# A decoder layer's first attention: three transposes by VectorE and a DRAM scratch in place of TensorE, and the output projection placed behind the diagonal blocks

## The reference

```python
q, k, v, g = x@Wq, x@Wk, x@Wv, x@Wg           # 16 heads; 64 columns of q and k, 128 of v and g a head
s = clip(x@Ws, -32, 32)                       # 64 slots a head
z = cumlogsumexp(s, time); p = exp(s - z); decay = exp(z_before - z)
hk = hk*decay + k (x) p;  ok = q*scale . hk   # a running state over the 512 tokens
pv = softmax(ok)                              # over the 64 slots
hv = hv*decay + p (x) v;  o = pv . hv
o  = o*rsqrt(mean(o*o)+eps)*g_norm*(g*sigmoid(g))
x  = layernorm(x + o@Wo)
```

## Time and profile before

| | us |
|---|---|
| median of 3 runs (1936.99 to 1939.8) | 1938.25 |
| profiled execution, whole | 1938.87 |
| profiled execution, span of the core | 1937.0 |
| PE busy in the span | 1905.9 (98%) |
| VectorE, ScalarE, POOL busy | 1235.6, 719.9, 555.9 |

### The profile page before, as it was taken

One profiled execution on the slowest core, in us unless ns is written; L12 is line 12 of the kernel. 1 busy time (PEld: TensorE's weight loads), 2 busy tenths in 40 slices (PEclk: granted clock), 3 DMA queues, 4 the chain that ended last, 5 costly groups with the idle time before them and its releaser, 6 DMA issues.

```text
span 1937.0 us, 30623 instructions
## 1 busy us (share of the span) xinstructions
PE 1905.9 (98%) x12099; PEld 1421.9 (73%) x12099; DVE 1235.6 (64%) x2107; ACT 719.9 (37%) x1819; POOL 555.9 (29%) x571
## 2 busy tenths in 40 slices
PE   9999999999999999999999989999999999999998
PEld 7888888888888888888888864444444468888876
DVE  4655555555555555555555678999999865555556
ACT  3222222222222222222222215888888832222122
POOL 2041151141141142142042243344242322223332
PEclk9999999999999999999999998999999999999999
DMA  5000100100001001001000001111110211111112
GB/s 174 1 1 12 39 11 2 39 12 24 16 12 39 1 12 39 1 12 39 1 12 4 6 2 26 27 27 27 27 27 20 34 19 22 30 20 30 20 17 87
DMA packets 124988, 47.08 MB, mean 24 GB/s; under 512 B 89264, under 2 KB 116400, under 8 KB 124848
## 3 DMA queue, kind: packets, MB, share of 16 engines
q1 hardware_dynamic: 124848, 45.14, 9.4%
HBM read 32.79 MB, written 4.19 MB: 19 GB/s over the span
## 4 chain that ended last, share of the span: by engine, by line
PE 92%; DVE 3%; ACT 3%; SPq 1%; issue 0%; DMA 0%; POOL 0%; POOLq 0%; DVEq 0%; ACTq 0%
PE a_ps L59 20%; PE a_ps L61 19%; PE a_ps L60 19%; PE a_ps L992 6%; PE a_ps L954 5%; PE a_ps L1008 5%; PE a_ps L1142 3%; PE a_ps L976 3%; PE a_ps L936 2%; ACT x_prob L1586 2%; PE a_ps L1087 2%; PE a_ps L1125 1%; PE a_ps L1068 1%; PE a_ps L1147 1%; PE a_ps L1130 1%; PE a_ps L1096 1%
## 5 line engine op out<-in xcount | busy, mean ns | idle before, releaser
L1650 DVE TENSOR_REDUCE a_raw_qks<-a_ps 128x1 f32<-128x512 f32 x512 | 320.9, 682 | 22.0 <-PE a_ps L954 21.3
L1586 ACT ACTIVATE x_prob<-a_ps 128x512 f32<-128x512 f32 x512 | 280.0, 609 | 63.4 <-PE a_ps L976 61.8
L1692 DVE SCALAR_TENSOR_TENSOR a_gate<-a_gate,a_ps 128x256 f32<-128x256 f32 x128 | 53.9, 421 | 264.0 <-ACT a_gate L1485 264.0
L1483 ACT COPY a_v<-a_ps 128x256 f32<-128x256 f32 x128 | 47.6, 372 | 436.5 <-PE a_ps L61 433.4
L59 PE MATMUL a_ps<-a_vg_hi,a_xT_lo 128*128 128x512 f32 x512 | 208.9, 408 | 0.0
L61 PE MATMUL a_ps<-a_vg_hi,a_xT_hi 128*128 128x512 f32 x512 | 200.9, 392 | 0.0
L60 PE MATMUL a_ps<-a_vg_lo,a_xT_hi 128*128 128x512 f32 x512 | 199.9, 391 | 0.0
L776 POOL TENSOR_TENSOR a_f<-a_rs 128x8 f32<-128x8 f32 x32 | 6.3, 198 | 569.9 <-ACT a_flat L1507 569.9
L59 PE MATMUL a_ps<-a_xT_hi,a_qks_lo 128*128 128x512 f32 x384 | 156.5, 408 | 0.4 <-DVE a_xT_lo L1681 0.4
L61 PE MATMUL a_ps<-a_xT_hi,a_qks_hi 128*128 128x512 f32 x384 | 150.0, 391 | 0.0
L60 PE MATMUL a_ps<-a_xT_lo,a_qks_hi 128*128 128x512 f32 x384 | 149.7, 390 | 0.0
(11 more groups left out here) (191 smaller groups left out, 4119.7 us busy)
## 6 DMA issues: line engine op xcount, KB each, us to landing
a_raw_vg<-in_L_attn_Wv_dram SPq DMA_DIRECT2D x8, 512.0 KB, 4.2
a_raw_vg<-in_L_attn_Wg_dram SPq DMA_DIRECT2D x8, 512.0 KB, 6.3
a_raw_qks<-in_L_attn_Wo_dram SPq DMA_DIRECT2D x8, 512.0 KB, 3.4
a_xT_lo<-a_xT_lo SPq DMA_DIRECT2D x32, 128.0 KB, 2.3
x_values<-acc SPq DMA_DIRECT2D x13, 256.0 KB, 2.8
acc<-in_x_dram SPq DMA_DIRECT2D x3, 1024.0 KB, 10.7
out_dram<-acc SPq DMA_DIRECT2D x6, 512.0 KB, 2.8
f_raw_down<-in_L_ffn_down_w_dram SPq DMA_DIRECT2D x44, 64.0 KB, 2.4
```

The lines of the kernel that those rows point to most:

```text
L1586: nc.scalar.activation(prob[par][:, s % 4, :], score_bank(q, s, par), ACT.Exp, scale=X_SCALE).then_inc(exp_done[par], 1)
L1650: nc.vector.tensor_reduce(nm[:, q % 2, i % 4, par, i // 4:i // 4 + 1], max_bank(u, q, i, par), AX.X, ALU.max, negate=True).then_inc(max_re ...
```

## The change

Transposes. For steps 1 to 31, e and the keys are no longer turned by PE. VectorE's transpose turns each block of 32x32 in place in one instruction (`turn_e` 512 columns, `turn_keys` 384). What is still missing is that the blocks change places; SP does that by writing to a DRAM tensor with four DMAs (one for each 32 rows, `put_blocks`) and reading it back with one (`get_blocks`), each waiting for the one before. ScalarE then reorders within a partition (`rows_of_e`, `rows_of_keys`). The gated output of steps 0 to 29 goes the same way in steps 1 to 30 (`turn_output`, 1024 columns; `put_og`, `get_og`, 512 KB each way; `high_turned` on ScalarE; `low_turned` on VectorE). Step 0's e and keys and the last two outputs stay with PE. SP's order within a step is put e, put keys, get e, put output, get keys, get output.

Order. On PE the projection K moves from behind the diagonal blocks to right behind S, and with it its copy on ScalarE; VG+3 comes ahead of the diagonal blocks and `project_out` behind them, ahead of Q. On VectorE `low_turned` stands ahead of the last gating, and `add_out` behind the masking of the diagonal blocks.

Weights. The factor of half the norm weight is multiplied into Wo by POOL (one more pass in `split_wo`), no longer into the output by ScalarE and VectorE; K and Q are split one by one; the load of Wo is issued in the fourth step of a pair.

The last two steps. Maxima of the second attention go to other PSUM banks; in `last_step` the eleven transposes of `keep_clock` ahead of `slots` and their wait are gone, and the row statistics of batch 2 are spread over that step instead of standing ahead of it.

The diff, cut to its core:

```diff
@@ SP, in place of the loop over pairs
+            def put_blocks(dram, turn, done):
+                for r in range(4):
+                    sp.dma_start(dram[:, :, r, :].rearrange("s j x -> j s x"),
+                                 turn[32 * r:32 * (r + 1), :, :, :].rearrange("j s i x -> j s (i x)")).then_inc(done, 16)
+            def get_blocks(dram, turn, done):
+                sp.dma_start(turn[:, :, :, :].rearrange("p s i x -> p (s i x)"),
+                             dram[:, :, :, :].rearrange("s j r x -> (s j) (r x)")).then_inc(done, 16)
+            def get_og(n):
+                sp.wait_ge(og_out, 64 * n)
+                get_blocks(og_blocks, og_turn, og_back)
...
+            for n in range(NSTEP - 1):
+                put_e(n + 1)
+                put_keys(n + 1)
+                get_e(n + 1)
+                if n:
+                    put_og(n)
+                get_keys(n + 1)
+                if n:
+                    get_og(n)
...
@@ PE, step
-                next_project(S)
+                next_project(S, K)
                 key_states(n)
...
-                if not first:
-                    out_rows(n)
                 next_project(VG + 2)
...
-                if not first:
-                    project_out(n, pair0, (0, 1, 2, 3))
                 next_project(VG + 3)
...
                 diagonals(n)
-                next_project(K)
+                if not first:
+                    project_out(n, pair0, (0, 1))
+                    project_out(n, pair0, (2, 3))
                 next_project(Q)
-                transpose_e(n + 1)
-                transpose_keys(n + 1)
                 values(n, j)
...
@@ PE, last_step
-                pe.wait_ge(og_ready, 2 * n)
-                keep_clock(5, ob[0])
                 key_states(n)
...
-                keep_clock(6, ob[0])
                 slots(n)
...
@@ ACT
+            def high_turned(n):
+                act.wait_ge(og_back, 16 * n)
+                wait(act, wo_done, 4 * (n - 1))
+                nc.scalar.copy(oT_hi[:, :, :].rearrange("p g (b i) -> p b g i", b=4),
+                               og_turn[:, :, :, :]).then_inc(oThi_ready, 1)
...
@@ DVE
+            def turn_output(n):
+                dve.wait_ge(ogs_ready, n)
+                wait(dve, oTlo_ready, oT_count(n - 1))
+                nc.vector.transpose(og_turn[:, :, :, :],
+                                    og[:, :, :].rearrange("p g (b r) -> p b g r", b=4)).then_inc(og_turned, 1)
+            def low_turned(n):
+                dve.wait_ge(oThi_ready, oT_count(n))
+                nc.vector.tensor_tensor(oT_lo[:, :, :].rearrange("p g (b i) -> p b g i", b=4), og_turn[:, :, :, :],
+                                        oT_hi[:, :, :].rearrange("p g (b i) -> p b g i", b=4).bitcast(F32),
+                                        ALU.subtract).then_inc(oTlo_ready, 1)
...
@@ DVE, step
                 clip(n + 1, b1)
+                turn_e(n + 1)
                 running_key_states(n)
                 running_states(n)
+                turn_keys(n + 1)
                 normalised_slots(n)
...
                 less_maxima(n)
+                if not first:
+                    turn_output(n)
                 gating(n + 1, VG + 1, b1)
                 slot_sum(n)
-                if not first:
-                    low_oT(n)
                 gating(n + 1, VG + 2, b1)
                 scaled_weights(n)
                 slot_reciprocals(n)
-                if not first:
-                    add_out(n, (j - 1) % B, (0, 1, 2, 3))
+                if not first:
+                    low_turned(n)
                 gating(n + 1, VG + 3, b1)
                 mask_diagonal_blocks(n)
+                if not first:
+                    add_out(n, (j - 1) % B, (0, 1))
+                    add_out(n, (j - 1) % B, (2, 3))
```

More of the change, by code:

```diff
@@ L286, in layer_program, with oT_count @@
         FAC = 5
+        TURNED = NSTEP - 2
+        def oT_count(n, h=1):
+            return n if n <= TURNED else TURNED + 2 * (n - TURNED - 1) + h + 1
         def each_pair(eng, step):
@@ L291, in each_pair, with turn_of @@
                 step(n, n // B, n % B, n == 0)
+        FIRST_ORDER = (S, VG, VG + 1, VG + 2, VG + 3, K, Q)
+        def turn_of(m, i):
+            return i if m else FIRST_ORDER.index(i)
         def at(n, k):
@@ L602, in place_keys @@
                         .then_inc(keys_in_place, 16)
[L604 to L610, removed]
+            ctx_rows = ctx_in.rearrange("b (t p) d -> p (b t) d", p=P)
+            for n in range(NSTEP - 1):
+                p, j = n // B + 1, n % B
+                if n == NSTEP - 3:
+                    sp.wait_ge(wo_ready, PAIRS)
+                    for q in range(2):
+                        get_rows(q, 0, q)
+                put_e(n + 1)
[6 more added lines that the diff above has]
+                    get_og(n)
+                if n == NSTEP - 2:
+                    place_keys(0, 0)
+                if j == 0 and p < PAIRS:
+                    sp.wait_ge(wo_ready, p)
+                    sp.wait_ge(vg_ready, p)
+                    load_s(sp, p)
+                    load_vgqk(sp, p)
+                if j == 3 and p < PAIRS:
+                    load_output(sp, p)
+            get_rows(2, 0, 2)
+            place_keys(1, 1)
+            get_rows(3, 0, 3)
             put_max_rows(0, 0)
@@ L1092, in states @@
                 pe.wait_ge(v_ready, 4 * n + 4)
-                pe.wait_ge(e_ready, n + 1)
+                wait(pe, sub_ready, n)
                 for i in range(TT - 1):
@@ L1108, in project_out @@
                 pe.wait_ge(wo_ready, pair + 1)
[L1109 removed]
+                pe.wait_ge(oTlo_ready, oT_count(n))
                 for t in tiles:
@@ L1286, in _ @@
                 keep_clock(4)
-            for i in range(PROJ):
+            for i in FIRST_ORDER:
                 project(0, i, 0, 0, prologue=True)
@@ L1852, in last_step @@
                 reduce_max(0, 0, 5)
+                statistics(n - 1, B - 3, (0,))
                 scaled_weights(n)
```

243 lines of the change are left out of this document (159 added, 84 removed).

## The result

The changed kernel takes 2062.0 us (median of 4 runs, 2061.2 to 2063.4) against 1937.9 for the kernel before (4 runs, 1937.0 to 1939.8): a ratio of 1.064, 95% interval 1.0621 to 1.0658. It is slower by 124 us. The forecast, 2017, had the sign and the main mechanism; it was 45 us too low, within its range.

What follows compares the result with a forecast made beforehand. PE, busy 98%, was taken to bound the kernel: 1938.9 - 50.0 (transposes) - 3 (last step) + 30 x (3.08 wait + 1.32 clock) = 2017.9, forecast 2017 us, range 1932 to 2090.

Steps and rivals of the forecast that it cites:

- matmuls that leave PE: Transposes dropped from PE: the output's 0.87 us in 30 steps, e's and keys' 0.77 in 31, together 50.0 us saved.
- last step: Statistics and clock-keeping transposes leave the path in the last step: between -6 and +3 us, taken as -3.
- wait for the output: PE idle ahead of project_out until low_turned is done: 3.08 us in each of 30 steps, bounds 2.5 to 5.3.
- clock behind the wait: PE at half clock after each wait: 1.32 us in each of 30 steps, with 0 and 3.42 as ends.
- What bounds it, and what leaves PE: PE, busy 98%, bounds the kernel; whatever it no longer does is gained in full unless something else makes it wait.
- When the output is wanted and when it is there: PE reaches project_out 22.56 us into the step; the output's low part, through DRAM, is there at 25.64.
- What is late next: Check of other engines' waits: e, keys and POOL's passes cost nothing; VectorE's lost slack 0 to 0.5 us, taken as 0.
- the slack that I called used up: VectorE's scan and two reciprocals, formerly 3.1 us ahead of the next step, now end with values: taken as 0 cost.
- the rival with the clock lost at every wait: Each of 30 waits ahead of project_out loses 3.42 us to half clock: 2080 us, chance 0.13.
- the rival with the wait but the clock kept: PE waits 3.08 us ahead of project_out in 30 steps without losing clock: 1978 us, chance 0.20.
- The covered trip: Rival: the output's DRAM trip ends before PE wants it, so no wait and a faster kernel: 1885 us, chance 0.16.
- the condition I named: For the covered trip, the output must be ready 7.60 us after less_maxima; the change breaks even at 9.4 us.

Runs made afterwards that it cites:

- experiment 3: Changed kernel with the gated output turned by PE again in all steps, e and keys still through DRAM: 1911.65 us, ratio 0.9858 to the kernel before.
- experiment 2: Changed kernel with POOL's splitting of the S, value and gate weights waiting until low_turned is done: 2034.6 us, ratio 1.0493 to the kernel before.
- experiment 1: Changed kernel with projection Q moved ahead of project_out on PE: 1970.4 us, ratio 1.016 to the kernel before.
- experiment 4: Changed kernel with 30 unread transposes of the identity ahead of project_out in steps 1 to 29: 2014.2 us, ratio 1.0391 to the kernel before.
- 9: Kernel of experiment 8 with the output's read issued ahead of the keys' read and its split ahead of the keys' copies on ScalarE: 1906.9 us, ratio 0.9841.
- Experiment 6: Kernel of experiment 2 with 30 unread transposes of the identity ahead of project_out in steps 1 to 29: 1987.3 us, ratio 1.0244 to the kernel before.
- 5: Changed kernel with both Q ahead of project_out and POOL's weight splitting behind low_turned: 1948.6 us, ratio 1.0045 to the kernel before.
- 7: Kernel of 5 with project_out writing the PSUM banks okb and tb, so values needn't wait for the additions: 1926.7 us, ratio 0.994.
- experiment 8: Kernel of 7 with the scan and the first of its two reciprocals ahead of low_turned on VectorE: 1905.2 us, ratio 0.9818; run again 1902.5 us.

## Why the prediction was right in sign and 45 us low

| term of the sum | forecast | measured | by |
|---|---|---|---|
| matmuls that leave PE | -50.0 | -0.74 a step for e and keys (forecast 0.77); the output's 0.87 not by itself | experiment 3 |
| last step | -3 | -4.2 | experiment 3 |
| wait for the output | +92.4 | +114.6 | the profile after |
| clock behind the wait | +39.6 | +56.6 in `project_out`; 56.7 by difference | the profile after; experiment 3 |
| step 30 | no term | +4.0 | the profile after; experiment 3 |

The 56.7 is a difference over steps 1 to 29, which take 1149.7 us in the changed kernel and 1003.6 in experiment 3: 146.1 + 29 x 0.87 - 114.6. Reading and difference agree. The 0.87 is the forecast's own figure.

- **What bounds it, and what leaves PE: right.** PE stood at 98% and what it no longer did was gained in full wherever it did not wait, at the clock of 1.00 (experiment 3, for e and the keys).
- **When the output is wanted and when it is there: right** link by link up to the last. The unknown of the trip, four writes of 128 KB at 2.5 and one read of 512 KB at 3.3, lay close to the rows taken for it. Outside the seven long steps and step 1 the wait was 3.35 on average, 3.08 by forecast.
- **`low_turned`: right 23 times, wrong 7 times.** This is the first step that failed. The price was taken from a VectorE pass of the same size, and POOL was let off under "What is late next" because it is busy 26%. A share of busy time can't say whether two instructions meet. POOL's list in order of time, with what releases it, would have shown it. This is before, POOL and VectorE, and was there to be read:

```profile
550.78 4.53 POOL L749 TENSOR_TENSOR a_vg_hi<-a_raw_vg,a_zero 128x2048 fp32r<-128x2048 f32 x1
...
550.68 1.23 DVE L1699 TENSOR_TENSOR_SCAN a_rz<-a_eT 128x512 f32<-128x512 f32 x1
```

  Two POOL passes of 4.5 us, one after the other, once in four steps. The first starts 27.7 us after its step's start, where `low_turned` was forecast from 24.4 to 25.6: by the list alone they miss each other. But POOL's splitting starts when VG+3 is done (25.3 after the step's start), and the change moves VG+3 ahead of `project_out`; in the changed kernel the pass starts at 24.1. That the two engines exclude each other shows here too, the other way round: the scan started 0.10 earlier, and POOL's pass took 4.53 where the same pass has 3.60 in the changed kernel. Against the forecast wait each hold added 6.16 - 3.08 = 3.08 us, 7 x 3.08 = 21.6; experiment 2 gives 27.4, of which 24.2 are wait.
- **The clock: right mechanism, too small a price.** This is the second step that failed, by 56.6 - 39.6 = 17 us. I interpolated by the length of the idle time between 1.50 (no loss) and 5.58 (3.42 lost), which gave 1.32 for 3.08. Measured: 6.87 to 8.4 us for a `project_out` of 5.57, 2.0 us on average for each of 28 waits, and with no relation to its length: a wait of 3.05 was followed by 7.14, one of 6.15 by 6.96 and one of 3.78 by 8.38. In the other kernels not even the loss itself goes by the length: 3.24 us cost nothing twice in seven times (experiment 1), 2.75 nothing three times in seven (4), 1.94 cost 1.6 and 2.17 nothing (9). What decides it is not shown. Experiments 4 and 6 show that it is idleness that costs the clock, and no property of the trip.
- **Late next: mostly right.** e and keys came in time in all steps, and the slack that I called used up cost nothing, since PE's wait gave it back. It did come due when the wait was taken away: the 0.87 ahead of `values` in experiments 1 and 5 and the held scan in 7.
- **The rivals.** What happened lies nearest to the rival with the clock lost at every wait (2080, with a chance of 0.13): it was lost behind all 28 waits of 2.87 us or more, but at 2.0 us each where that rival had 3.42. Experiment 6 is the rival with the wait but the clock kept: 1987, forecast 1978. The covered trip, forecast 1885, is what experiment 8 comes nearest to, 1902 to 1905, but it needed four edits besides: the condition I named, the output ready in 7.60 us, can't be met by this trip, which takes 10.5 from the end of `less_maxima` (589.66) to that of a `low_turned` of 1.22 (600.12); it has to be given more cover.

What stays open: the spread of the usual waits (2.87 to 4.87), which I put down to the DMAs' landings without a run on it; what decides whether an idle time of 1.9 to 3.3 us costs the clock; why step 30 is 4.0 us longer; and whether POOL's two passes could be cut or placed so that neither `low_turned` nor the scan meets them, which wasn't tried.

## What to carry to other kernels

A transfer through DRAM costs an engine nothing when its result is wanted a step later, and when it is wanted in the same step all that the cover does not reach: price the trip from the last producer to the first consumer, and put the wait's clock loss beside it, as a price for each wait that does not grow with its length (1.3 to 2.9 us here, 2.0 on average) and that waits of 1.9 to 3.3 us paid in some steps and not in others. For each VectorE instruction that is moved, or whose operand moves from PSUM to SBUF, look at what POOL does at that moment, in order of time and over a whole period of the loop, not at its busy share. When a wait is filled with later work, ask what that work was covering.

## What the runs showed that I had not expected

- VectorE and POOL stop each other for whole instructions: `low_turned`, 1.22 us alone, took 4.50 and the scan, also 1.22 alone, 5.34, both ending 1.08 us after POOL's pass; POOL's passes took 5.42 in place of 4.59 and 4.53 in place of 3.60 where VectorE came first.
- Thirty matmuls whose result nobody reads, put into each wait, make the kernel faster by 48 us (experiment 4, 2062.0 to 2014.2).
- The same idle time of 3.24 us ahead of the same matmuls was followed by a granted clock of 1.00 in two steps and of half speed in five (experiment 1).
- A read of 192 KB issued 0.38 us behind one of 512 KB went with a longer landing of the larger, 3.6 us against 3.3.
